# A hybrid attention and mixture-of-experts block: reordering the second routed pass's front and its last sums

## The reference

```python
x = L0_attn_a_x
x = x + _L0_attn_a_ref(_layernorm(x), W_q, W_k, W_v)                 # normalised q, k; mean of k*v over the rows
x = x + _L0_ffn_ref(_layernorm(x), gate_w, gate_b, sh_w1, ...)      # first expert pass
x = x + _L0_attn_b_ref(_layernorm(x), qkv_w, qkv_b, out_w, out_b)   # softmax attention, 16 heads of 8
x = x + _L0_ffn_ref(_layernorm(x), gate_w, gate_b, sh_w1, ...)      # second expert pass

# inside _L0_ffn_ref(x): TOP_K = 2, 8 experts, hidden width 512
router_probs = softmax(x @ gate_w + gate_b)
expert_values, expert_indices = top_k(router_probs, k=2)
expert_values = expert_values / (sum(expert_values) + 1e-09)
all_outputs = gelu(x @ ew1[e] + eb1[e]) @ ew2[e] + eb2[e]            # for every expert e
weights_E = (one_hot(expert_indices) * expert_values[..., None]).sum(axis=2)
return x + _mlp(x, sh_w1, sh_b1, sh_w2, sh_b2) + einsum('bse,bsed->bsd', weights_E, all_outputs)
```

## Time and profile before

| | |
|---|---|
| Median of 3 runs | 814.87 us (811.92 to 815.82) |
| The profiled execution's own time | 809.36 us |
| Its span in the profile | 807.5 us |
| PE busy | 660.6 us (82%) |
| DVE busy | 626.6 us (78%) |
| ACT busy | 523.9 us (65%) |
| POOL busy | 496.0 us (61%) |
| Mean granted PE clock | 0.931 |

### The profile page before, as it was taken

The page is one execution under the profiler, slowest core; times in us unless marked ns, Lnnn a source line. Parts: engine busy times, 40 slices in busy tenths (PEclk is TensorE's granted clock), DMA queues, the critical chain, the costliest instruction groups (busy, mean ns, idle before and its releaser), DMA issues.

```text
span 807.5 us, 22799 instructions
## 1 busy us (share of the span) xinstructions
PE 660.6 (82%) x7807; PEld 476.5 (59%) x7808; DVE 626.6 (78%) x1404; ACT 523.9 (65%) x1255; POOL 496.0 (61%) x512
## 2 busy tenths in 40 slices
PE   0666399699999946898988899889978989999980
PEld 0343389588988943343433444443447978898870
DVE  6589979477777637999999899999855277878848
ACT  4666764276666634687888788878865556666640
POOL 4997516677887068678248828107877727777730
PEclk9999589799999976699999999999989999999995
DMA  7232210133335411101000100000111323323236
GB/s 206 66 92 33 78 29 1 27 82 89 83 89 78 63 43 39 25 11 41 6 2 15 41 2 1 2 2 16 47 57 53 113 63 84 89 80 87 71 110 208
DMA packets 52505, 46.88 MB, mean 58 GB/s; under 512 B 8771, under 2 KB 44779, under 8 KB 52440
## 3 DMA queue, kind: packets, MB, share of 16 engines
q1 hardware_dynamic: 43352, 28.02, 12.4%
q0 software_dynamic: 9088, 17.98, 9.1%
HBM read 26.76 MB, written 20.13 MB: 58 GB/s over the span
## 4 chain that ended last, share of the span: by engine, by line
PE 48%; DVE 24%; POOL 10%; ACT 8%; issue 7%; DMA 2%; SPq 1%; DVEq 0%; ACTq 0%; POOLq 0%
PE ps L930 23%; PE ps L1074 13%; DVE mx L2371 9%; POOL rows L868 7%; PE ps L1089 3%; PE ps L1325 3%; PE ps L1166 2%; DVE xres L2249 2%; ACT xn L1458 2%; ACT scratch L1665 1%; DVE hlo L2364 1%; DVE hhi L2358 1%; DVE stats L1767 1%; ACT hl L1467 1%; DVE rnorm L1821 1%
## 5 line engine op out<-in xcount | busy, mean ns | idle before, releaser
L1545 ACT ACTIVATE h<-ps,b1T 128x256 f32<-128x256 f32 x440 | 172.1, 480 | 56.6 <-PE ps L930 56.6
L2371 DVE TENSOR_REDUCE mx<-ps 128x2 f32<-128x512 f32 x256 | 171.4, 684 | 16.0 <-PE ps L930 14.9
L1665 ACT ACTIVATE scratch<-ps 128x512 f32<-128x512 f32 x256 | 152.4, 613 | 36.0 <-PE ps L930 34.6
L930 PE MATMUL ps<-xg,w1s 128*128 128x256 f16 x936 | 117.4, 276 | 11.1 <-issue 9.5
L1074 PE MATMUL ps<-w2s,hhi 128*128 x1248 | 117.2, 219 | 0.0
L879 POOL DMA_INDIRECT ytok<-yst,didx x78 | 89.4, 1146 | 42.4 <-DVE yst L2183 21.4
L930 PE MATMUL ps<-kst,qst 32*128 32x256 f16 x512 | 98.1, 286 | 17.1 <-DVE mx L2371 13.5
L769 POOL DMA_INDIRECT scratch<-rows,tok_i x78 | 90.3, 1157 | 26.8 <-issue 23.2
L930 PEld LDWEIGHTS ps<-xg,w1s 128*128 x936 | 88.5, 99 | 25.1 <-issue 14.8
L1571 ACT ACTIVATE xg<-ps 128x512 f16<-128x512 f16 x78 | 46.6, 598 | 83.2 <-PE ps L1166 83.1
L2125 DVE SCALAR_TENSOR_TENSOR hlo<-h,hhi 128x1024 f16<-128x1024 f32 x78 | 95.6, 1226 | 2.7
(11 more groups left out here) (317 smaller groups left out, 1372.6 us busy)
## 6 DMA issues: line engine op xcount, KB each, us to landing
gy<-rows SPq DMA_DIRECT2D x39, 136.0 KB, 2.2
ysorted<-yst SPq DMA_DIRECT2D x39, 128.0 KB, 1.8
h<-in_L_ffn_ew SPq DMA_DIRECT2D x16, 256.0 KB, 3.2
scratch<-ytok SPq DMA_DIRECT2D x16, 256.0 KB, 3.6
xres<-in_L_attn_a_x SPq DMA_DIRECT2D x4, 512.0 KB, 5.6
rows<-hl SPq DMA_DIRECT2D x4, 512.0 KB, 3.1
out_x<-xres SPq DMA_DIRECT2D x4, 512.0 KB, 4.3
scratch<-rows,tok_i POOLq DMA_INDIRECT x78
```

Source lines behind the costliest of these rows:

```text
L930: return pe.matmul(o, a, b, start=start, stop=stop)
L1545: last = act.activation(h32[:, u % 2, f], HB[u % 2][:, f], ACT.Gelu_apprx_tanh, bias=b1T[:, ds(e * CH + c, 1)], scale=1.0 / PS)
L1665: act.activation(prb[:, (s // 4 * 4 + (s + 2) % 4) % 8, :], ps[:, s % 2, :], ACT.Exp, scale=HD ** -0.5 / (PS * PS))\
L2371: dve.tensor_reduce(mx[:, c, j:j + 5:4], ps[:, 2 + s % 2, :].rearrange("p (n k) -> p n k", n=2), AX_X, ALU.max).then_inc(Att.mx, 1)
```

## The change

In the second pass's front, PE turns the last four batches and computes their logits right after the first two `up_shared`, ahead of the first `down_shared`; ACT copies them right after the first gelu; DVE makes the choice before it takes out any shared result, and the places and the table after only one. Both calls of `Route.weights` move from behind the front and from the end to DVE's front, after shared results 4 and 7, and ACT's exponential for them from its end to after gelu 5. At the end, DVE starts to combine after shared result 13; results 14 and 15 are taken out after the first and the second step. The output's last store of four batches is cut in two.

```diff
+    STORES = ((0, 4), (4, 4), (8, 4), (12, 2), (14, 2))
-            for g in range(NG):
-                sp.wait_ge(moe[1].last, GT * (g + 1))
-                sp.dma_start(batches(od, g), batches(xrows, g)).then_inc(stored, 16)
-            sp.wait_ge(stored, 16 * NG)
+            for first, n in STORES:
+                sp.wait_ge(moe[1].last, CB * (first + n))
+                sp.dma_start(od[:, ds(first, n), :], xrows[:, ds(first, n), :]).then_inc(stored, 16)
+            sp.wait_ge(stored, 16 * len(STORES))
...
                     up_shared(0)
                     up_shared(1)
-                    down_shared(0)
-                    up_shared(2)
                     for b in range(GB * g, NBATCH):
                         if b >= GB * g + 2:
                             pe.wait_ge(Post.xT, b - 1)
...
                     last.then_inc(Post.logits, 1)
-                    down_shared(1)
+                    down_shared(0)
+                    up_shared(2)
                     up_shared(3)
-                    down_shared(2)
-                    up_shared(4)
                     post_rank(RANK3, 2)
                     pe.wait_ge(Post.summed, 3)
                     mm(USED3, ones16[:, :], msum[:, 2, :], True, True).then_inc(Post.rank, 1)
+                    down_shared(1)
+                    up_shared(4)
+                    down_shared(2)
...
                     gelu_shared(0)
-                    gelu_shared(1)
                     for b in range(first, NBATCH):
                         act.wait_ge(Post.turned, b - first + 1)
                         post_copy(TB[b % 2], b)
-                    for n in range(2, SA):
+                    for n in range(1, SA):
                         gelu_shared(n)
+                        if n == 5:
+                            post_exp(2)
...
-                if r == 1:
-                    post_exp(2)
...
                     post_last()
-                    result_shared(0)
-                    result_shared(1)
                     dve.wait_ge(Post.logits, 1)
                     Route.first(2, GATE3.rearrange("p (t e) -> p t e", e=E))
                     Route.second(2)
                     Route.third(2)
-                    result_shared(2)
+                    result_shared(0)
                     dve.wait_ge(Post.rank, 1)
                     Route.placed(2, RANK3)
                     Route.table()
-                    for n in range(3, SA):
+                    for n in range(1, SA):
                         result_shared(n)
+                        if n == 4:
+                            Route.weights(0, 1)
+                        if n == 7:
+                            Route.weights(2, 2)
...
                     last_group_beside_shared()
-                    Route.weights(0, 1)
                     scattered()
-                    for n in range(SA, NS):
+                    for n in range(SA, NS - 2):
                         result_shared(n)
-                    Route.weights(2, 2)
                     for f in range(NC):
                         if f == 0:
+                            dve.wait_ge(m.y, 2 + NBLK + SA)
+                        if f == SA // 2:
                             dve.wait_ge(m.y, 2 + NBLK + NS)
                         combine_loaded(f)
+                        if f < 2:
+                            result_shared(NS - 2 + f)
```

## The result

| | before | after |
|---|---|---|
| Median of 16 runs each | 811.56 us (806.95 to 816.12) | 807.71 us (801.46 to 811.55) |
| Ratio, 95% interval | | 0.9941 (0.9919 to 0.9964), that is -4.8 us (-6.6 to -2.9) |
| The profiled execution's own time | 809.36 us | 808.51 us |
| Span in the profile | 807.5 us | 806.7 us |
| PE, DVE, ACT, POOL busy | 660.6, 626.6, 523.9, 496.0 us | 664.0, 628.6, 524.2, 497.2 us |

The kernel is faster by 0.6%; -3.2 us was forecast. The ratio and its interval are worked out from all runs and are not the quotient of the two medians, which is 0.9953, or -3.85 us; the later ratios are of the same kind. The two profiled spans differ by only 0.8 us, since one execution lies up to 6 us off its kernel's median. So I compare stretches inside the second pass, counted from its first `up_shared` (before at 601.96, after at 604.13), not spans.

What follows compares the result with a forecast made beforehand. Second pass bound by POOL's sends until 649.9 us, then PE through 39 blocks, then DVE's sums. End -4.4 (sums -3.7, store -0.7) plus front +1.2 gave -3.2: 814.87 to 811.7 us, range 808.3 to 815.0.

Steps and rivals of the forecast that it cites:

- Taken off the median, 814.87 - 3.2 = 811.7: Whole kernel: the forecast -3.2 us subtracted from the median of the runs shown, 814.87, giving 811.7 us.
- +1.2: PE's front: the clock falls near 610, returns near 615.5, making PE's end 651.3; +1.2 us, bounds 0 and +2.9.
- POOL sends without pause; 0 gained: Front: the choice made some 5 us sooner gains 0, since POOL does not wait for `slot_i`.
- Sums, -3.7: End: DVE's sums start at 781.6 instead of 786.32 and end at 800.5 instead of 804.2, -3.7 us.
- Last store, -0.7: End: the last store carries 256 KB, not 512; gain between 0 and 1.45 us, the middle taken, -0.7.
- The sends' lengths, 0: Front: DVE's moved instructions could stretch POOL's sends; 0 taken, bounds -0.3 (the table's stretch vanishes) and +0.8 us.
- ACT's two table loads, 0 or +0.2: ACT's front: switch and exponential take 2.8 us, costing 0 or +0.2; rival with costlier loads: 812.4 us, chance 0.05.
- The new wait for shared result 1: PE's front: `down_shared` 3 waits for shared result 1 behind DVE's table, starting 622.8 instead of 622.19; cost 0.
- The clock that stays up: Rival: the clock does not fall in the front, leaving -4.4 us, 810.5 us; chance 0.31.
- Less from the end: Rival: crowded early loads or a halved store landing no sooner lose 1.5 us, 813.2 us; chance 0.12.
- The clock that stays down: Rival: holes in PE's front keep the clock down; 819.0 us if until 630, 821.5 if until 635; chance 0.08.
- the first turn of a block 6 us behind the last: Sign at the front's end: the first turn of a block comes 6 us behind POOL's last send.

Runs made afterwards that it cites:

- e5: The kernel before, unchanged, profiled once more on a quick chip; one run, 809.78 us.
- e14: The kernel before, unchanged, profiled a third time; one run, 810.72 us.
- e8: Against the kernel before, on a quick chip: end and stores as changed, weights and exponential in the front, front order kept; 807.26 us, 0.9958.
- e15: Against the kernel before: end and stores as changed, weights and exponential in the front, front order kept, profiled again; one run, 803.96 us.
- e16: Against the kernel before: only the weights and their exponential moved into the front, on a quick chip; one run, 808.16 us.
- e10_fill: Against the kernel after, on a quick chip: 17 unread matmuls added in the holes of PE's front; 803.38 us, 0.9918 of the kernel before.
- e7: The kernel after, unchanged, repeated on a quick chip; 806.14 us, 0.9951 of the kernel before.
- e2_end_only: Against the kernel before, on the slow chip: end and stores as changed, weights and exponential in the front, front order kept; 936.02 us, 1.0013.
- e9_front_only: Against the kernel before, on a quick chip: only the new front order; weights, exponential, end and stores kept; 809.64 us, 1.0002.
- e13_end_fill: Against e2_end_only: 18 unread matmuls added on PE around the first turns of a block, old front order kept; 804.68 us, 0.9927 of the kernel before.
- e13: Short for e13_end_fill: old front order, end as changed, 18 unread matmuls on PE; 804.68 us, 0.9927 of the kernel before.
- e1_again: The kernel after, unchanged, repeated on the slow chip; 935.06 us, 0.9971 of the kernel before.

## Why the prediction was wrong

The forecast was 811.7 us and its range ended at 808.3; the median is 807.71. Three steps failed: the base of the sum, and two terms of the front. By the range alone the first would do.

1. **"Taken off the median, 814.87 - 3.2 = 811.7."** The median of three runs was 3.3 us above that of sixteen, 811.56, and runs of one kernel spread over 9 to 10 us. The forecast's difference off the better base gives 808.4, and its range moved along, 805.0 to 811.7, holds 807.71. The text itself had the warning, "5.5 us under the median of the runs shown", and used it only to choose the higher base. As a difference, -3.2 lies inside the measured -6.6 to -2.9.

2. **"+1.2" for the front, taken in full to the end.** Its mechanism was right. Forecast were a fall near 610 and a return near 615.5, in the new trace's time some 2.2 later (the first `up_shared` at 604.13 instead of 601.96); the fall stood between 612.6 and 619.5, a little longer. The forecast's end of PE's front, 651.3, is 49.3 from its first `up_shared`; measured 49.58, and 49.51 to 49.78 in the other new fronts. The first turn came 1.4 to 2.0 us later than in before, e5 and e8. What I missed is behind it. PE's wait for POOL at the end of the old front was itself a price: in four of six executions the clock fell there. From the last send to PE's last product the six old fronts took 139.87, 140.98, 140.93, 141.17, 139.62 and 140.48, mean 140.5, and the four new ones 141.45, 141.18, 141.30 and 141.14, mean 141.3: +0.8 instead of +1.2. The last send also starts 0.24 sooner (41.75 on the mean of four, against 41.99 in before, e5 and e8).

3. **"POOL sends without pause; 0 gained."** This held in the one trace that the forecast had and in e5 and e8. In e14, e15 and e16 POOL waited 2.3 to 3.2 us for `slot_i`, and the last send came 2.3 to 3.2 us later; no new front has this wait. I had judged the slack of the choice, one us, from one execution. With this term the front is worth +0.4 us where POOL would not have waited and -2.3 where it would; on the mean of the six old and four new profiles it is -0.9 (183.0 against 183.9), in place of +1.2. Ten profiles are few for such a mean, and its sign hangs on how often POOL waits.

The other terms stood:

- **Sums, -3.7.** Their start moved from 2.57 behind PE's last product to 1.7 to 2.2 before it; forecast was 4.7 (786.32 to 781.6), measured 4.3 to 4.8. They last 18.7 to 19.0 us instead of 17.89, for a forecast of 1.0 more: two results, and a load late by 0.3. Net -3.5 in the kernel after (17.00 - 20.46).
- **Last store, -0.7.** Measured -0.8, in the middle of the bounds: 2.9 us for 512 KB, 2.1 for 256 KB. With it the end is -4.2 (19.52 - 23.75), -4.4 to -4.6 in e7, e8 and e15.
- **The sends' lengths, 0.** The bound "-0.3 (the table's stretch vanishes)" is what came: 35.08 against 35.42. The long send remains, under the same DVE instruction; the Trainium skill (GPSIMD Engine Reference, 1. Specifications) has POOL contend with DVE instructions of two SBUF inputs, and 1.96 us for 0.96 agrees. None of the sends was stretched by `weights` to a sum that shows.
- **ACT's two table loads, 0 or +0.2.** The exponential starts 0.01 us after its load and the gelu 0.01 after the second. The drain of 1.38 us behind each load that the Trainium skill gives (ScalarE: Activation LUTs, What ACT_TABLE_LOAD costs) does not show; the measurement decides, and that rival is out. The switch and the exponential took 2.9 us, for a forecast of 2.8.
- **The new wait for shared result 1.** It is there, 0.17 us before the `down_shared` at 627.09. Forecast was 0.7 with the clock up. In e10_fill the clock is up and the wait is 0.16 all the same, so the term was too large by about 0.5.
- **Rivals.** The clock that stays up: refuted in this front, and e10_fill shows what it would be worth. Less from the end: refuted, the only wait of more than 0.2 us for loads is the first (e2_end_only, on the slow chip, is the exception). The clock that stays down: refuted, it came back by 619.5, and after 10 us in the longest case, e7. The sign "the first turn of a block 6 us behind the last" send did not come: it is 7.6 to 7.8 us, as the forecast's own 651.3 already implied more than 6.

The sum, as the traces have it: -4.3 (end) and, in the front, +0.4 where POOL would not have waited or -2.3 where it would, that is -3.9 to -6.6 us and -5.2 on the mean of the profiles. The measured interval is -6.6 to -2.9. The times alone can't tell these from -3.2: e8_end_only and e9_front_only give -3.4 and +0.2, each with 2 us to either side. That the end makes the gain is shown by both, times and traces; that the front costs little or gives something back rests on the traces.

Two versions gained more on the kernel before than the change did. e10_fill, the change with 17 fillers in the front, ran 0.9918 of before; e13_end_fill, the old front with the new end and 18 fillers, 0.9927. Their intervals overlap each other and that of the kernel after, so that either beats the kernel after isn't shown by the times; what speaks for e10_fill is the 2.3 us that its trace shows against e7_again.

## What to carry to other kernels

Reordering to make one result earlier puts small dependent pieces next to each other on PE, and the holes between them can cost the clock for several times their length; keep a full piece of work among them, or fill the holes with products that nobody reads. Removing a wait further down may give a part of it back, so cost an edit to the next place where another engine is waited for, and look at the clock there too. Profile the kernel before more than once before a slack of one us is called a slack: here one trace showed no wait for the choice, and three others of the same order showed 2.3 to 3.2 us. Build the forecast of a 0.5% change as a ratio, since the median of three runs is no base for a time that has to be right within 3 us.

## What was not expected of the hardware

- The clock can fall twice within 50 us, for different holes: in e5_before_look it is down from about 599 to 606, back at 1.00, and falls again behind 650. In the kernel after the two falls lie some 10 us apart, near 602.2 and 612.5, with only 3 us at 1.00 between.
- A clock that stays up at first saves nothing if the next piece must wait anyway. In e7_again it was at 1.00 for both `up_shared`, 2.78 us in place of 5.21, and PE then waited 3.80 us for DVE's `hl` and lost the clock over that longer hole:

```profile
602.53 2.78 PE L931 MATMUL ps<-xT,w1s 128*128 128x256 f16 x24 [0.61 <-DVE xres L2402]
609.11 1.03 PE L1016 MATMUL ps<-ident,hl 128*128 128x128 f16 x8 [3.80 <-DVE hl L2049]
```

```profile
602.60:606.20 3.60, 2.71 (x24) 2.17 (x23) 3.09 (x17) 1.78 (x3) 2.69 (x4) 1.00 0.18 63
606.60:617.00 10.40, 6.94 (x67) 6.20 (x68) 5.77 (x18) 6.14 (x13) 7.96 (x9) 0.54 0.16 54
```

  Its front still ended at 49.78. In e13 to e16, with the old order, the same start ended worse: POOL then waited for the choice.
- One chip ran the kernels in 931 to 941 us where others took 803 to 812. Its chain names a releaser that the profile can't place. Its mean granted clock is 0.85 to 0.89 in place of 0.91 to 0.94; in e1_again it is at 0.50 for 41 us from 615 on and for 20 us from 677 on, and PE's idle time before L931 that is put down to issue is 44.7 us, beside 10.0 in the kernel after. By an estimate from the two mean clocks (0.880 of 931.7 us, 0.924 of 806.7) the clock can make up some 50 of the 125 us at most. What lies behind it stays open. What also stays open is why the old front's fall comes in some executions and not in others, with waits of much the same length.
